# A fused cross-attention and expert-FFN kernel: the first LayerNorm's transposed tokens are loaded channels-first and completed by a row, instead of being normalised, transposed and copied

## What is computed

```
q, k, v = LN(x) Wq' + bq,  ctx Wk' + bk,  ctx Wv' + bv
x  = x + softmax(q k' / sqrt(128)) v                   # one batch at a time
h  = LN(x);  probs = softmax(h router');  a = gelu(h w1' + b1) w2' + b2
k_tok = argmax(a) + 1;  keep the k_tok largest probs of the 8 experts as scores
x  = x + sum_e score_e * ((silu(h gate_e') * (h up_e')) down_e')     # 8 experts, 336 hidden each
```

## Time and profile before

| | us |
|---|---|
| median of 3 runs (lowest, highest) | 787.82 (786.17, 788.01) |
| the profiled execution | 788.26 |
| its span, first to last instruction | 786.5 |
| TensorE matmul busy | 764.4 (97%) |
| VectorE busy | 621.9 (79%) |
| ScalarE busy | 585.6 (74%) |
| GpSimd busy | 563.3 (72%) |
| mean granted TensorE clock | 0.991 of full |

### The profile page before, as it was taken

The page is one execution under the profiler, slowest core; times in us unless marked ns, Lnnn a source line. Parts: engine busy times, 40 slices in busy tenths (PEclk is TensorE's granted clock), DMA queues, the critical chain, the costliest instruction groups (busy, mean ns, idle before and its releaser), DMA issues.

```text
span 786.5 us, 13918 instructions
## 1 busy us (share of the span) xinstructions
PE 764.4 (97%) x3825; PEld 384.1 (49%) x3825; DVE 621.9 (79%) x1341; ACT 585.6 (74%) x1032; POOL 563.3 (72%) x629
## 2 busy tenths in 40 slices
PE   7779999999999999999999999999999999999997
PEld 4534445554545545454554545455454545544443
DVE  6679888787887878778787877878687786878765
ACT  5777877777777777777778777778777777777664
POOL 2876877868686776868668685876868587686763
PEclk9979999999999999999999999999999999999999
DMA  9000011102010110201101020110201001010100
GB/s 345 6 15 0 14 28 14 41 1 67 2 46 21 27 42 1 66 0 26 40 19 47 0 66 0 26 40 0 66 0 49 19 15 28 1 41 1 28 1 27
DMA packets 52382, 25.07 MB, mean 32 GB/s; under 512 B 32496, under 2 KB 51056, under 8 KB 52336
## 3 DMA queue, kind: packets, MB, share of 16 engines
q1 hardware_dynamic: 52048, 24.06, 11.9%
q10 hardware_dynamic: 288, 0.48, 0.2%
HBM read 12.73 MB, written 4.19 MB: 22 GB/s over the span
## 4 chain that ended last, share of the span: by engine, by line
PE 88%; DVE 4%; POOL 3%; issue 2%; ACT 2%; DMA 1%; POOLq 0%; DVEq 0%; ACTq 0%
PE bank L497 26%; PE bank L499 26%; PE bank L498 26%; PE bank L409 2%; PE bank L389 2%; POOL weighted L1025 1%; PE bank L493 1%; PE bank L398 1%; DVE bank L1313 1%; PE bank L482 1%; PE bank L375 1%; PE bank L454 1%; PE bank L467 1%; DVE hid_lo L1319 1%; PE bank L473 1%
## 5 line engine op out<-in xcount | busy, mean ns | idle before, releaser
L1025 POOL TENSOR_TENSOR weighted<-silu,score_bc 128x512 f32<-128x512 f32 x336 | 424.5, 1270 | 167.7 <-ACT silu L792 163.2
L1313 DVE SCALAR_TENSOR_TENSOR bank<-bank,h_scale,weighted 128x512 f32<-128x512 f32 x336 | 253.1, 753 | 122.7 <-PE bank L499 109.9
L786 ACT ACTIVATE hid_hi<-bank 128x512 f16<-128x512 f32 x336 | 200.6, 597 | 145.7 <-DVE bank L1313 144.7
L792 ACT ACTIVATE silu<-bank,silu_scale 128x512 f32<-128x512 f32 x336 | 230.4, 686 | 24.2 <-PE bank L499 23.6
L1319 DVE TENSOR_TENSOR hid_lo<-bank,hid_hi 128x512 f16<-128x512 f32 x336 | 228.2, 679 | 11.8 <-ACT hid_hi L786 11.8
L497 PE MATMUL bank<-xn_lo,gate_hi 128*128 128x512 f16 x336 | 128.5, 382 | 0.9 <-POOL xn_lo L959 0.9
L497 PE MATMUL bank<-xn_lo,up_hi 128*128 128x512 f16 x336 | 128.3, 382 | 1.0 <-DVE hid_lo L1319 0.9
L497 PE MATMUL bank<-hid_lo,down_hi 128*128 128x512 f16 x336 | 127.5, 380 | 1.7 <-DVE down_lo L1140 1.5
L499 PE MATMUL bank<-xn_hi,gate_hi 128*128 128x512 f16 x336 | 128.4, 382 | 0.0
L498 PE MATMUL bank<-xn_hi,gate_lo 128*128 128x512 f16 x336 | 128.3, 382 | 0.0
L498 PE MATMUL bank<-xn_hi,up_lo 128*128 128x512 f16 x336 | 128.3, 382 | 0.0
(11 more groups left out here) (175 smaller groups left out, 831.3 us busy)
## 6 DMA issues: line engine op xcount, KB each, us to landing
x_in<-in_x SPq DMA_DIRECT2D x16, 256.0 KB, 2.9
out<-out_sb SPq DMA_DIRECT2D x16, 256.0 KB, 2.4
ctx_in<-in_ctx_t SPq DMA_DIRECT2D x14, 240.0 KB, 2.8
raw_gate<-in_gate_t SPq DMA_DIRECT2D x3, 448.0 KB, 6.4
raw_up<-in_up_t SPq DMA_DIRECT2D x3, 448.0 KB, 8.1
raw_down<-in_down_t SPq DMA_DIRECT2D x3, 448.0 KB, 10.0
out_sb<-in_ctx_t SPq DMA_DIRECT2D x2, 240.0 KB, 5.1
consts_sb<-in_consts ACTq DMA_DIRECT2D x1, 403.0 KB, 3.7
```

Of the source, the lines that this page charges most:

```text
L786: af(hid_hi[j % HRING][:], up_bank[j % U_BANKS][:], ACT.Copy).then_inc(hid_hi_ready, 1)
L792: af(silu[j % RING][:], gate_bank[(par + j) % G_BANKS][:], ACT.Silu, scale=silu_scale[:])\
L1025: g.tensor_tensor(weighted[j % RING][:], silu[j % RING][:], score_bc[par][:], ALU.mult)\
L1313: v.scalar_tensor_tensor(up_bank[j % U_BANKS][:], up_bank[j % U_BANKS][:], h_scale[:], weighted[j % RING][:], ALU.mult, ALU.mult).then_inc ...
```

## The change

A second copy of the input, `x_t` (channels on partitions), is an input of the kernel. From block 2 on:

- `turn_x`, `turned_x` and `norm1` are gone. `xn_t` is now x_t + (std - mean), that is std * (LN(x) + 1), where std - mean is one number per token.
- `rstd_1` on GpSimd computes std = (variance+eps) * rstd, and std - mean in `row`, one small instruction more than before. `rstd1` has two buffers.
- SyncE loads `xt_in` (`load_xt`), stores `row` (128 partitions of 16 bytes) to a DRAM scratch of 2 KB, waits for it, and reads it back broadcast to all 128 partitions as `row_bc` (`spread_row`).
- GpSimd adds the two (`add_row`, at j=14 of turn t for block t+3; block 2's at j=6 of turn 0, ahead of `rstd_1`). `row_bc` is read with a step of 4 elements.
- `row_below` becomes four VectorE instructions, (energy - maximum) * rstd, one per batch.
- `xn_nat` and `below` of blocks 0 and 1 lie in the last two blocks of `x2_all`.

```diff
             def load_xt(n):
+                wait(sp, xnt_ready, n)
+                sp.dma_start(xt_in[:], xt_blocks[n]).then_inc(xt_loaded, 16)
+            def spread_row(n):
+                sp.wait_ge(ln1_shift, n + 1)
+                wait(sp, row_in, 16 * (n - 2))
+                sp.dma_start(row_kept.rearrange("o (p b) -> (o p) b", b=BB), row[:]).then_inc(row_stored, 16)
+                sp.wait_ge(row_stored, 16 * (n - 1))
+                wait(sp, xnt_ready, n)
+                sp.dma_start(row_bc[:], row_kept.broadcast_to([P, NT])).then_inc(row_in, 16)
...
                 if by_dma:
                     turned(xn_lo[1 - par], xn2_lo).then_inc(halves_in[1 - par], 16)
+                if isinstance(t, int) and t == 0:
+                    spread_row(2)
+                if is_block(t + 3):
+                    load_xt(t + 3)
+                    spread_row(t + 3)
                 if is_block(t + 1):
                     sp.wait_ge(spread_lo_ready, t + 1)
...
@@ TensorE: turn_x, energies, turn
-                if dst is x0:
-                    wait(pe, x2_ready, n)
-                    if isinstance(n, int) and n == 2:
-                        pe.wait_ge(bc_ready, 1)
...
-                if isinstance(n, int) and n == 1:
-                    pe.wait_ge(x2_ready, 1)
+                if isinstance(n, int) and n == 2:
+                    pe.wait_ge(bc_ready, 1)
+                wait(pe, x2_ready, n)
...
-                    if j == 4 and is_block(t + 2):
-                        turn_x(t + 2)
@@ ScalarE: turn
-                    if isinstance(t, int) and t == 0 and j == 2:
-                        norm1(2, 0, 0, BB)
...
-                    if j == 5 and is_block(t + 2):
-                        turned_x(t + 2)
...
-                    if j == 13 and is_block(t + 3):
-                        norm1(t + 3, nxt, 0, 2)
-                    if j == 14 and is_block(t + 3):
-                        norm1(t + 3, nxt, 2, BB)
@@ GpSimd: rstd_1, add_row, turn
+                if by_row:
+                    g.tensor_tensor(std1[:], ve1[:], rstd1[par][:], ALU.mult).then_inc(ln1_std, 1)
+                    pool.wait_ge(ln1_std, n - 1)
+                    g.tensor_tensor(row[:], std1[:], less1[:], ALU.add).then_inc(ln1_shift, 1)
...
+            def add_row(n):
+                pool.wait_ge(xt_loaded, 16 * (n - 1))
+                pool.wait_ge(row_in, 16 * (n - 1))
+                pool.wait_ge(e_done, n)
+                g.tensor_tensor(xn_t[:].rearrange("p (b n) -> p b n", b=BB),
+                                xt_in[:].rearrange("p (b n) -> p b n", b=BB),
+                                row_bc[:].rearrange("p (n b) -> p b n", b=BB), ALU.add).then_inc(xnt_ready, 1)
...
                     if j == 6 and is_block(t + 3):
-                        rstd_1(t + 3)
+                        if isinstance(t, int) and t == 0:
+                            add_row(2)
+                        rstd_1(t + 3, nxt)
+                    if j == 14 and is_block(t + 3):
+                        add_row(t + 3)
@@ VectorE: row_below
+                for b in range(BB):
+                    last = v.tensor_scalar(below_kept[:, b, :], x0[:, b * CTX:(b + 1) * CTX], row_top[:, b:b + 1],
+                                           rstd1[par][:, b:b + 1], ALU.subtract, ALU.mult)
+                last.then_inc(below_ready, 1)
```

More of the change, by code:

```diff
@@ L71, with program @@
 FIRST_DOWN = 7
-def program(nc, x, ctx_t, consts, consts16, gate_t, up_t, down_t, out):
+def program(nc, x, x_t, ctx_t, consts, consts16, gate_t, up_t, down_t, out):
     x_blocks = x.rearrange("(t b p) d -> t p b d", b=BB, p=P)
     out_blocks = out.rearrange("(t b p) d -> t p b d", b=BB, p=P)
+    xt_blocks = x_t.rearrange("p (t n) -> t p n", n=NT)
     ctx_blocks = ctx_t.rearrange("p (t n) -> t p n", n=NC)
+    row_kept = nc.dram_tensor("row_kept", (1, NT), F32, kind="Internal").ap()
     with ExitStack() as stack:
@@ L139, in program @@
         less1, less2 = sb("less1", [P, BB]), sb("less2", [P, BB])
-        rstd1, rstd2 = sb("rstd1", [P, BB]), sb("rstd2", [P, BB])
-        shift1, shift2 = sb("shift1", [P, BB]), sb("shift2", [P, BB])
-        xn_nat, xn2_nat = sb("xn_nat", [P, BB, P]), sb("xn2_nat", [P, BB, P])
+        rstd1, rstd2 = [sb(f"rstd1_{k}", [P, BB]) for k in range(2)], sb("rstd2", [P, BB])
+        std1, shift1, shift2 = sb("std1", [P, BB]), sb("shift1", [P, BB]), sb("shift2", [P, BB])
+        xn2_nat = sb("xn2_nat", [P, BB, P])
         xn_t, xn2_t = sb("xn_t", [P, NT]), sb("xn2_t", [P, NT])
@@ L148, in program @@
         row_top = sb("row_top", [P, BB])
-        below = sb("below", [P, NC])
+        xt_in, row_bc = sb("xt_in", [P, NT]), sb("row_bc", [P, NT])
+        row = sb("row", [P, BB])
+        below_kept = sb("below_kept", [P, BB, CTX])
+        xn_nat, below = x2_all[:, BLOCKS - 2], x2_all[:, BLOCKS - 1].rearrange("p b d -> p (b d)")[:, 0:NC]
         probs = sb("probs", [P, BB, CTX])
@@ L198, in program @@
         w_hi_done, w_lo_done, warm_ready = [sem(f"w_hi_done{n}") for n in range(9)], sem("w_lo_done"), sem("warm_ready")
-        ln1_stats, ln1_mv, ln1_ve, ln1_less, ln1_rstd, ln1_shift, xn_ready = (
-            sem(n) for n in ("ln1_stats", "ln1_mv", "ln1_ve", "ln1_less", "ln1_rstd", "ln1_shift", "xn_ready"))
+        ln1_stats, ln1_mv, ln1_ve, ln1_less, ln1_rstd, ln1_std, ln1_shift, xn_ready = (
+            sem(n) for n in ("ln1_stats", "ln1_mv", "ln1_ve", "ln1_less", "ln1_rstd", "ln1_std", "ln1_shift", "xn_ready"))
         wq_chain, key_done, key_ready = sem("wq_chain"), sem("key_done"), sem("key_ready")
@@ L326, in _ @@
                 load_x(n, n % 2)
+            load_xt(2)
             def turned(dst, src):
@@ L745, in exps @@
                 wait(act, sum_ready, n)
-                af(probs[:].rearrange("p b n -> p (b n)"), below[:], ACT.Exp).then_inc(exp_done, 1)
+                af(probs[:].rearrange("p b n -> p (b n)"),
+                   below if isinstance(n, int) and n < 2 else below_kept[:].rearrange("p b n -> p (b n)"), ACT.Exp)\
+                    .then_inc(exp_done, 1)
             def router_exps(n):
@@ L920, in over, with rstd_1 @@
                 return col.unsqueeze(2).broadcast_to([P, BB, n])
-            def rstd_1(n):
+            def rstd_1(n, par):
+                by_row = not isinstance(n, int) or n >= 2
                 pool.wait_ge(ln1_mv, n + 1)
-                wait(pool, xn_ready, n)
+                if by_row:
+                    pool.wait_ge(below_ready, n - 1)
+                    wait(pool, row_in, 16 * (n - 2))
+                else:
+                    wait(pool, xn_ready, n)
                 g.tensor_tensor(ve1[:], mv1[:, :, 1], eps_sb[:], ALU.add).then_inc(ln1_ve, 1)
@@ L1042, in turn @@
                     if isinstance(t, int) and t == 0 and j == 0:
-                        rstd_1(2)
+                        rstd_1(2, 0)
                     if isinstance(t, int) and t == 0 and j == 2:
@@ L1060, in turn @@
                         rstd_2(t + 2)
-            rstd_1(0)
-            rstd_1(1)
+            rstd_1(0, 0)
+            rstd_1(1, 1)
             rstd_2(0)
@@ L1180, in norm1 @@
                 for b in range(BB):
-                    last = v.tensor_scalar(xn_nat[:, b, :], x_in[par][:, b, :], mv1[:, b, 0:1], rstd1[:, b:b + 1],
+                    last = v.tensor_scalar(xn_nat[:, b, :], x_in[par][:, b, :], mv1[:, b, 0:1], rstd1[par][:, b:b + 1],
                                            ALU.subtract, ALU.mult)
@@ L1197, in row_max, with row_below, early_below @@
                     .then_inc(top_ready, 1)
-            def row_below(n, src=x0):
+            def row_below(n, par):
+                dve.wait_ge(top_ready, n + 1)
+                dve.wait_ge(exp_done, n)
+                for b in range(BB):
+                    last = v.tensor_scalar(below_kept[:, b, :], x0[:, b * CTX:(b + 1) * CTX], row_top[:, b:b + 1],
+                                           rstd1[par][:, b:b + 1], ALU.subtract, ALU.mult)
+                last.then_inc(below_ready, 1)
+            def early_below(n, src=x0):
                 dve.wait_ge(top_ready, n + 1)
                 wait(dve, exp_done, n)
-                v.tensor_tensor(below[:].rearrange("p (b n) -> p b n", b=BB),
+                v.tensor_tensor(below.rearrange("p (b n) -> p b n", b=BB),
                                 src[:, 0:NC].rearrange("p (b n) -> p b n", b=BB),
@@ L1333, in turn @@
                     if j == 8 and is_block(t + 2):
-                        row_below(t + 2)
+                        row_below(t + 2, par)
                     if j == 8 + late(t) and is_block(t + 1):
@@ L1417, in _ @@
             row_max(0)
-            row_below(0)
+            early_below(0)
             values(0, up_bank[2])
@@ L1433, in _ @@
             actor_arg(0)
-            row_below(1)
+            early_below(1)
             actor_gelu(0)
@@ L1497 @@
         "x": np.asarray(x).reshape(BATCHES * P, P),
+        "x_t": np.asarray(x).reshape(BATCHES * P, P).T,
```

10 lines of the change are left out of this document (7 added, 3 removed).

## The result

The changed kernel takes 803.53 us (median of 4 runs, 802.71 to 804.60), the kernel before beside it 787.91 (786.17 to 788.13). The ratio is 1.0207, 95% interval 1.0188 to 1.0226. Forecast was 782.4 in a range of 780.2 to 785.6: the sign was wrong. The profiled execution took 802.71, its span is 800.9, 14.4 us more than before.

The account below looks back on a forecast made before the run. TensorE's stream was taken to bound the kernel. Gains of 4.4 (turns 4 to 13), 0.0 (turns 1 to 3) and 1.0 (turn 0) made 5.4 us, giving a median of 782.4 us, range 780.2 to 785.6.

Parts of the forecast that it names:

- Part 1: TensorE's four transposes go: 0.44 us per full-clock turn, 4.4 us over turns 4 to 13.
- What bounds the kernel: TensorE's stream is the span; other engines have 0.58 us of room in turns 4 to 13, none in 1 to 3.
- Part 3: VectorE's row_below at j=8 as four instructions: +0.43 us per turn, fitting the late turns' room, cancelling the early turns' gain.
- Rival A: VectorE's four row_below instructions take 0.34 us each, +0.8 per turn, giving 786.1 us; chance 10%.
- Part 4: GpSimd's add_row at j=14 takes 1.27 us, holds scores 0.1 us, caught up by j=16: price 0.
- Rival D: VectorE's row_below waits for GpSimd as count_far does, costing 1.25 us per turn, giving 792.3 us; chance 6%.
- Part 2: ScalarE loses norm1 (1.64 us) and turned_x: worth nothing in steady turns, 1.0 us in turn 0.
- Part 5: Three more transfers per turn; row store and broadcast take 5 to 20 us, read 17 us later: price 0.
- Part 6: Turn 0 gains 1.0 us (loss of 0.5 to gain of 2); energies of block 2 waits 1.2 for add_row.
- Early turns: Turns 1 to 3: no room at gate of tile 14, so row_below's 0.43 us eats the 0.44; gain nothing.

Follow-up runs that it names:

- a6: Changed kernel with two rows per token, GpSimd multiplying and adding at j=10, and the old one-instruction row_below: 785.37 us, ratio 0.998.
- b1: Kernel before with row_below from block 2 on as four tensor_scalar, nothing else: 795.68 us, ratio 1.012.
- b2: Kernel before with one more GpSimd addition at j=14, the size and 16-byte step of add_row, its output unread: 801.57 us, ratio 1.0184.
- a1: Changed kernel with add_row on GpSimd at j=9 instead of j=14: 789.45 us, ratio 1.003.
- a3: Changed kernel with keys of block t+3 at j=19 instead of j=18: 787.34 us, ratio 1.001.
- a9: Changed kernel with result on VectorE at j=16 instead of j=17: 789.68 us, ratio 1.003.
- a8: Changed kernel with two rows per token, old row_below, keys at j=19 and block 2's rows applied at j=4 of turn 0: 778.12 us, ratio 0.9879.

## Why the prediction was wrong

- **Part 1, the transposes' price**: right. 0.44 us per turn; a6 shows it bare, 46.63 to 46.19.
- **What bounds the kernel**: this is the step that failed. I read TensorE's waits, found 1.1 us behind VectorE, and took "the tightest place" from the tile pipeline alone, 0.58 us at up of tile 13. Slack was measured only at gate and up, the consumers that repeat, and there it was read rightly: 0.68 of delay met 0.58 of room, and TensorE lost 0.1. `keys`, once per turn, waits for `result` with 0.08 us already lost, but the profile puts that wait down to "issue", so it showed in no row that names VectorE. Looking through the code for every semaphore that TensorE waits for from VectorE, and comparing ends with starts for each, would have found it: the two rows were 0.11 us apart.
- **Part 3, row_below**: mis-sized and misjudged. I took 4 x 0.25 from a `scalar_tensor_tensor`; four measured 1.25, +0.68 and not +0.43. The row of a single instruction is 0.39, not 0.34. That it "fits into the 0.58" failed with the step above: b1 alone costs 0.70 per turn. Of that, 0.56 was paid at `keys` and 0.12 at up of tile 13. Rival A had 0.8 for it, but spent it at up of tile 13.
- **Part 4, GpSimd**: the larger miss. I had `scores` held by 0.1 us at a price of 0. It was held by 0.24, and then caught by the `weigh` product that starts just after `rank_over`, another 0.76; from start to start on VectorE the two make 1.09. I had the row that shows such a catch, `count_far` at 1.00 against 0.18, and used it only for `row_below`, which was not caught. The 0.48 of `scores` in the earlier trace rows was such a catch too (0.19 without GpSimd), and I did not see it. b2 measures this part alone: 1.11 per turn. `add_row` itself took 1.53 where I took 1.27; the 16-byte step costs 0.26. The Trainium skill's rule (GPSIMD Engine Reference, Performance pitfalls for Q7 kernels) has the direction and not the size here: an estimated 1.9 by its cycles, 1.53 measured with one of two inputs at that step, and 1.56 in b2; the measurement decides.
- **Rival D's mechanism** was the right one on the wrong instruction, and I gave slower 6%. `row_below`, which reads PSUM, was kept out of it: 1.24 us in turn 0 of a1, beside a GpSimd product, and of a3, without one. The Trainium skill (SBUF — State Buffer, Who interferes with whom) says that a VectorE instruction with two SBUF inputs contends with a GpSimd instruction that reads SBUF; `scores` has two such inputs, and its 0.32 in a1 against 1.24 in after agrees.
- **Part 2, ScalarE**: right that its relief isn't worth anything in steady turns: its busy time fell by 27 us, unseen in the span. **Part 5, DMA**: right. The store of the row landed in 1.4 us and the broadcast in 3.9, against my 5 to 20 for the pair, and nothing in the loop waited for them at j=14.
- **Part 6, turn 0**: not settled. In this execution the gain was 1.67 to the `probs_transposes` of turn 0, `energies` of block 2 stood 0.93 for `add_row`, near the 1.2 forecast, and the second half gave 1.45 back. But a1, a3 and a9, which have the same start, reach that point at 75.45 to 76.03 and stand 0.5 to 2.4 there. The granted clock differs too: in 30 to 40, 40 to 50 and 50 to 60 us it was 0.79, 0.84 and 0.69 of full before, and 1.00, 0.88 and 0.77 after. That the forecast comes near is in part luck.
- **Early turns**: forecast 0.0, measured a loss of 0.78 in each of turns 1 and 2, from the same 1.77 us. In turn 1 TensorE lost 0.68 at gate of tile 14, the place and the mechanism that part 3 had forecast with 0.43, and 0.53 more before up of tiles 17 to 19 (their low halves end 0.06 before their readers), against the 0.44 of the transposes.

## What to carry to other kernels

When an engine has a stretch without idle time, every late microsecond reaches its end, so list each consumer of that end, also those that wait once per block and for a buffer rather than for data; a wait that the profile calls "issue" is a place to compare with the code. Before adding an instruction to a helper engine, look at what stands behind it in order, and at what the other engine will start next to: the same GpSimd addition cost 1.1 us per turn at j=14 and nothing at j=9. And where the extra work can go to an engine with idle time and nobody behind it, twice the work there (a6, with VectorE's old `row_below`) beats half of it at a full stretch.

## What the runs showed of the hardware

- A `tensor_scalar` of 128x120 float32 from PSUM with two pointer scalars, four in a row, held VectorE 0.31 each (347.75 to 349.00); the one `tensor_tensor` of 128x480 with a broadcast column held it 0.57 for the same 480 columns. The profile has the four at 383 to 397 ns each.
- GpSimd's `tensor_tensor` of 128x512 float32 took 1.53 us (1.519 to 1.537 in 14) with one input read at a step of 16 bytes, against 1.27 for `weigh`, which has no such read. `weigh` multiplies and `add_row` adds, but a multiplication with that step took 1.52 as well (a8).
- A 32-column `scalar_tensor_tensor` with both inputs in SBUF took 0.19 us with GpSimd idle. It took 0.32 when it began 1.00 us after the start of a GpSimd product (a1), 0.48 at 0.84 (before) and 1.24 at 0.07 (after), and it ended 0.05 after that product each time. I had not expected so small an instruction to decide 10 us.
- A 2 KB store in pieces of 16 bytes landed in 1.4 us, and 2 KB read back broadcast to 128 partitions in 3.9, against 2.7 for a plain load of the same 256 KB.
